# A graph network in one program: the fourth dense tile of a chunk is built in the attention stage instead of the message stage

## The reference

```python
h = relu(layernorm(x)); x = x + L0(h)   # messages: agg[src] += h[dst] * filter(edge) * cut
h = relu(layernorm(x)); x = x + L1(h)   # attention: softmax over the edges of each dst
h = relu(layernorm(x)); x = x + L2(h)   # graph convolution with degree norms
h = relu(layernorm(x)); x = x + L3(h)   # two weighted convolutions: out[dst] += ew * h[src]
```

## Time and profile before

| what | value |
|---|---|
| median of 3 runs | 5158.31 us (5143.35 to 5161.18) |
| the profiled execution | 5153.6 us, span 5151.8 us |
| mean granted TensorE clock | 0.901 of full |
| busy share of the span | PE 80%, PEld 68%, POOL 66%, DVE 59%, ACT 35% |
| message stage, about 130 to 1785 us | PE 1390.94, DVE 1155.84, ACT 965.19, POOL 1281.80 us busy; clock 0.94; DMA share 0.83 |
| attention stage, about 1985 to 3065 us | PE 893.86, DVE 819.86, ACT 419.71, POOL 774.95 us busy; clock 0.83; DMA share 0.23 |

### The profile page before, as it was taken

The page is one execution under the profiler, slowest core; times in us unless marked ns, Lnnn a source line. Parts: engine busy times, 40 slices in busy tenths (PEclk is TensorE's granted clock), DMA queues, the critical chain, the costliest instruction groups (busy, mean ns, idle before and its releaser), DMA issues.

```text
span 5151.8 us, 85066 instructions
## 1 busy us (share of the span) xinstructions
PE 4103.2 (80%) x25393; PEld 3526.8 (68%) x25393; DVE 3026.5 (59%) x10842; ACT 1786.2 (35%) x4226; POOL 3385.3 (66%) x3028
## 2 busy tenths in 40 slices
PE   2988888888888654888888885788876999869997
PEld 1665666556666454777777774666675999869996
DVE  3786666667667536777777764444444444434445
ACT  2665555555555433333333433222222000100001
POOL 0777777777777815777777735767644777457773
PEclk8999999999999876888888877999997999989998
DMA  6898888788888642222222212211115887567884
GB/s 202 210 208 182 183 187 178 177 185 186 182 185 187 129 109 65 56 55 55 54 55 55 54 29 66 53 49 50 49 31 206 287 294 281 179 229 281 291 294 155
DMA packets 516297, 768.12 MB, mean 149 GB/s; under 512 B 139247, under 2 KB 430680, under 8 KB 502520
## 3 DMA queue, kind: packets, MB, share of 16 engines
q0 software_dynamic: 189696, 201.26, 21.8%
q10 hardware_dynamic: 128128, 383.42, 20.3%
q1 hardware_dynamic: 198008, 177.89, 12.8%
HBM read 545.25 MB, written 217.03 MB: 148 GB/s over the span
## 4 chain that ended last, share of the span: by engine, by line
PE 40%; DMA 19%; issue 17%; DVE 12%; POOL 7%; DVEq 2%; SPq 1%; ACT 1%; POOLq 0%; ACTq 0%
DMA sums<-G,idx 18%; PE psCD L1330 8%; PE psF L1330 7%; POOL sums L741 7%; PE psCD L1249 5%; PE psCD L1303 3%; PE psA L1239 3%; PE psE L1303 3%; PE psCD L1315 3%; PE psF L1315 3%; DVE S L1881 2%; DVE G L1790 1%; PE psCD L1254 1%; DVEq L509 1%; DVE early L1870 1%
## 5 line engine op out<-in xcount | busy, mean ns | idle before, releaser
L716 POOL DMA_INDIRECT G<-table,idx x1352 | 1283.6, 949 | 778.6 <-issue 598.7
L741 POOL DMA_INDIRECT sums<-G,idx x832 | 1312.7, 1578 | 444.9 <-issue 203.6
L698 POOL DMA_INDIRECT G<-table,idx x832 | 785.8, 945 | 288.6 <-issue 252.0
L1187 PE MATMUL psB<-arena 128*128 128x300 f32 x1664 | 581.4, 482 | 251.8 <-ACT stage L909 213.3
L1187 PEld LDWEIGHTS psB<-arena 128*128 128x128 f32 x1664 | 317.4, 213 | 435.7 <-issue 304.1
L1330 PE MATMUL psCD<-arena,stage 128*128 128x192 f32 x2548 | 438.6, 330 | 0.0
L1330 PE MATMUL psF<-arena,stage 128*128 128x192 f32 x2548 | 431.3, 326 | 0.0
L828 ACT ACTIVATE arena<-psB,dinv 128x128 f32<-128x128 f32 x84 | 23.0, 378 | 1172.2 <-PE psB L1109 1160.5
L1330 PEld LDWEIGHTS psCD<-arena,stage 128*128 128x128 f32 x2548 | 419.6, 193 | 0.0
L1330 PEld LDWEIGHTS psF<-arena,stage 128*128 128x128 f32 x2548 | 411.8, 190 | 0.0
L909 ACT COPY stage<-psB 128x300 f32<-128x300 f32 x832 | 325.3, 426 | 239.4 <-PE psB L1187 233.2
(11 more groups left out here) (293 smaller groups left out, 8386.3 us busy)
## 6 DMA issues: line engine op xcount, KB each, us to landing
arena<-adjacency ACTq DMA_DIRECT2D x104, 2400.0 KB
adjacency<-stage ACTq DMA_DIRECT2D x416, 300.0 KB
acc<-in_src_row SPq DMA_DIRECT2D x104, 512.0 KB
arena<-in_dst_row SPq DMA_DIRECT2D x104, 512.0 KB
G<-table,idx POOLq DMA_INDIRECT x2184
sums<-G,idx POOLq DMA_INDIRECT x832
sums<-arena SPq DMA_DIRECT2D x4, 3300.0 KB, 25.5
table<-stage SPq DMA_DIRECT2D x28, 448.0 KB, 3.0
```

Of the source, the lines that this page charges most:

```text
L698: pool.indirect_dma_start(G[st.r][:, t * width:(t + 1) * width], None, tables[n], bass.IndirectOffsetOnAxis(ap=idx[st.r][:, t:t + 1], axis ...
L716: pool.indirect_dma_start(G[at.r][:, t * D:(t + 1) * D], None, tables[n], bass.IndirectOffsetOnAxis(ap=idx[at.r][:, t:t + 1], axis=0)).the ...
L741: pool.indirect_dma_start(sums_dram[t % SUMS], bass.IndirectOffsetOnAxis(ap=idx[st.r][:, t:t + 1], axis=0), G[st.r][:, t * TW:(t + 1) * TW ...
L1187: M.matmul(build_ps_1[q], lo, keys[:, q * HKEYS:(q + 1) * HKEYS], start=True, stop=True).then_inc(built["counted"], 1)
```

## The change

`AHEAD` becomes 3. In the message stage one `early_tile_hots`, two `early_half` products, two `early_half_kept` copies and one `early_tile_stored` per chunk go away, and `early_tile_stored(2)` takes the place of `early_tile_stored(3)` behind the first copy of the next turn. In the attention stage each turn gets one pair of one-hots, two half products, two copies and one store. The late tile uses buffers that are free in that stage: `lohots` and `keyhots` for the one-hots, `kept_2` in the arena, and one PSUM bank (`psB[:, 0:HKEYS]`) for both halves in turn, so the second product waits for the copy of the first. The numbers of tiles, bytes and sums over the whole program stay as they are.

```diff
-AHEAD = 4
+AHEAD = 3
...
+        kept_2 = [arena[:, behind + 5 * CHUNK + k * KEYS:behind + 5 * CHUNK + (k + 1) * KEYS] for k in range(RING)]
+        build_ps_2 = psB[:, 0:HKEYS]
...
+        def late_tile(c, j):
+            return CHUNKS * AHEAD + c * (DENSE - AHEAD) + j
...
             walk(act, general, l0["over"],
-                 [(low_sums_kept, 1), (early_tile_stored(3), 1), (filter_ssp, 0), (high_sums_kept, 1),
+                 [(low_sums_kept, 1), (early_tile_stored(2), 1), (filter_ssp, 0), (high_sums_kept, 1),
                   (early_half_kept(0, 0), 0), (early_half_kept(0, 1), 0), (keep_rows, 0), (early_tile_stored(0), 0),
-                  (early_half_kept(1, 0), 0), (early_half_kept(1, 1), 0), (early_half_kept(2, 0), 0), (early_half_kept(2, 1), 0), (early_tile_stored(1), 0),
-                  (early_half_kept(3, 0), 0), (early_half_kept(3, 1), 0), (early_tile_stored(2), 0)],
+                  (early_half_kept(1, 0), 0), (early_half_kept(1, 1), 0), (early_half_kept(2, 0), 0), (early_half_kept(2, 1), 0), (early_tile_stored(1), 0)],
...
             walk(act, general, l1["added"],
-                 [(diagonals, 0), (exps, 1), (onehot_turned, 0), (node_sums, 1)],
+                 [(diagonals, 0), (late_half_kept(0, 0), 1), (exps, 1), (onehot_turned, 0), (late_half_kept(0, 1), 1),
+                  (late_tile_stored(0), 1), (node_sums, 1)],
...
+            def late_half(j, q):
+                def stage_(st):
+                    b = late_tile(st.c, j)
+                    pe.wait_ge(built["hot"], b + 1)
+                    pe.wait_ge(built["kept"], 2 * b + q)
+                    M.matmul(build_ps_2, lohots[b % 2], keyhots[b % 2][:, q * HKEYS:(q + 1) * HKEYS],
+                             start=True, stop=True).then_inc(built["counted"], 1)
...
-                  (filter_two, 0), (early_half(2, 0), 0), (early_half(2, 1), 0), (early_half(3, 0), 0), (early_half(3, 1), 0)],
+                  (filter_two, 0), (early_half(2, 0), 0), (early_half(2, 1), 0)],
...
             walk(pe, general, l1["added"],
-                 [(per_edge, 1), (masked_scores, 0), (sums_turned, 2), (weighted_rows, 1)],
+                 [(per_edge, 1), (masked_scores, 0), (sums_turned, 2), (late_half(0, 1), 1), (weighted_rows, 1),
+                  (late_half(0, 0), 0)],
...
-                  (same_source, 0), (early_tile_hots(2), 0), (messages, 0), (early_tile_hots(3), 0)],
+                  (same_source, 0), (early_tile_hots(2), 0), (messages, 0)],
...
             walk(dve, general, l1["added"],
-                 [(new_maxima, 1), (window_onehot, 0), (exponents, 1), (weights, 1), (merge, 2), (largest, 0)],
+                 [(new_maxima, 1), (window_onehot, 0), (late_tile_hots(0), 0), (exponents, 1), 
+                  (weights, 1), (merge, 2), (largest, 0)],
```

More of the change, by code:

```diff
@@ L926, in early_tile_stored, with late_half_kept, late_tile_stored, stage_ @@
                 return stage_
+            def late_half_kept(j, q):
+                def stage_(st):
+                    b = late_tile(st.c, j)
+                    half_kept(b, q, kept_2, build_ps_2)
+                return stage_
+            def late_tile_stored(j):
+                def stage_(st):
+                    tile_stored(late_tile(st.c, j), st.c, AHEAD + j, kept_2)
+                return stage_
             def all_stored(tiles_built):
@@ L1004, in _ @@
             walk(act, general, l1["added"],
-                 [(diagonals, 0), (exps, 1), (onehot_turned, 0), (node_sums, 1)],
+                 [(diagonals, 0), (late_half_kept(0, 0), 1), (exps, 1), (onehot_turned, 0), (late_half_kept(0, 1), 1),
+                  (late_tile_stored(0), 1), (node_sums, 1)],
                  [], [diagonals, onehot_turned, exps, node_sums], 1)
+            with act.If(general > 0):
+                pass
+            with act.Else():
+                all_stored(CHUNKS * DENSE)
             def dense_kept(n):
@@ L1657, in early_tile_hots, with late_tile_hots, stage_ @@
                 return stage_
+            def late_tile_hots(j):
+                def stage_(st):
+                    b = late_tile(st.c, j)
+                    tile_hots(b, bass.ds(st.c * TILES + AHEAD + j, 1), (lohots[b % 2], keyhots[b % 2]))
+                return stage_
             dve.wait_ge(sums_clear, 16 * SUMS)
```

## The result

The changed kernel takes 5068.33 us (median of 4 runs, 5063.92 to 5071.42) beside 5153.64 us (5143.35 to 5161.18) for the kernel before: a ratio of 0.9835 [0.9814, 0.9856], some 85 us faster. Of these 22 us, 15 are the attention stage, which was forecast to lose them and did not move. In the message stage the sum came out, but not from the parts that it was added up from: the main item was priced too high by about as much as another, put at nothing, was worth.

The account below looks back on a forecast made before the run. The prediction took POOL's scatters and their landings to bound the message stage. It summed -83 us there and +15 us in the attention stage to -68 us, forecasting 5090 us, range 5025 to 5165.

Parts of the forecast that it names:

- the main item: Message stage: loads released 0.69 us sooner shorten the scatters' wait, 0.6 us per chunk.
- What bounds the kernel: Message stage: POOL's scatters and their landings set the pace, 16.1 us per chunk, 1.35 us above POOL's own.
- First item: Message stage: without the pair the loads issue 0.69 us sooner, saving 0.6 us per chunk, bounds nothing to 1.1.
- The products and copies lie beside the wait for the scatters and save nothing by themselves: Message stage: removing two products (1.25 us) and two copies (0.86 us) per chunk saves nothing by itself.
- Second item: Message stage: a scatter no longer lengthened by the pair beside it saves 0.1 us per chunk, bounds 0 and 0.22.
- Third item: Message stage: one store fewer ahead of the critical scatter saves 0.1 us per chunk, bounds 0 to 0.90.
- The sum: Message stage: the three savings make 0.8 us per chunk, 83 us over 104 chunks, bounds 0 and 141 us.
- The attention stage (+15 us): Attention stage: added late work takes the mean turn from 10.26 to 10.4 us, +15 us, bounds -6 and +46.
- Rival A: Attention stage: POOL loses each pair's whole 0.69 us, +43 us, taking back the message stage's gain; 5159 us, chance 0.14.
- B: Message stage nearly reaches POOL's own pace (-125 us) and the attention stage's clock stays up; 5027 us, chance 0.16.
- C: Message stage: loads ahead of the last scatter lengthen its landing; 5285 us, or 5203 with a third; chance 0.06.
- D: Message stage: the wait hangs on the loads whenever they come, so the shift changes nothing; 5163 us, chance 0.08.

Follow-up runs that it names:

- delay back: Changed kernel with one PSUM copy, about as long as the pair of one-hots, at the pair's old place in the message stage: 5065.11 us, ratio 0.9815.
- products back: Changed kernel with the fourth tile's two products and two copies back in the message stage, without its own pair or store: 5123.28 us, ratio 0.9946.
- pair back: Changed kernel with a fourth pair of one-hots back in the message stage, into a buffer that nobody reads: 5087.66 us, ratio 0.9860.
- loads sooner: Changed kernel with the duplicate sums ahead of the next window's one-hot in the message stage, releasing the loads earlier: 5107.38 us, ratio 0.9894.
- pair behind the weights: Changed kernel with the attention stage's late pair of one-hots behind the weights instead of behind the window's one-hot: 5067.24 us, ratio 0.9827.

## Why the prediction came out

**What bounds the kernel:** right. POOL's scatters and their landings set the message stage; their idle time fell and with it the whole time.

**First item, the loads released sooner (0.6 us): by itself worth nothing.** The loads did move, by 0.70 us in the turn (from 8.53 us behind ScalarE's release in the earlier trace rows to 7.83 us, the median after). But "delay back" undoes just that and costs nothing. The turn of the earlier trace rows that ran on pace with its loads 1.07 us ahead was read as showing what the loads do, but its last store was also far off, 3.15 us ahead of the scatter (issued at 1047.41). The place of the loads does go with the wait: in the five kernels with over 20 such chunks, those with loads just behind the last scatter and no late store wait 0.52 to 0.86 us, and in the changed kernel 75 of 80 chunks are no longer of that kind. What took them away was not the 0.69 us alone. A waiting turn can also keep them there: it lets ScalarE go by a landing, from which POOL's last scatter follows 8.27 us and the loads 8.53 us later. Which of the two comes first is not shown.

**"The products and copies lie beside the wait for the scatters and save nothing by themselves": this step failed.** Put back, they bring back 0.58 us per chunk, nearly all of the idle time. A way is seen in the trace: ScalarE, which makes the copies, also issues the stores, and a copy ahead of a store can delay it. Before, and with products back, a store leaves ScalarE within 1.5 us ahead of the chunk's last scatter in 51 and 50 of 80 chunks, in the changed kernel in 4. That scatter lands 8.12 and 8.29 us after its start in the chunks with such a store, and 7.38 and 7.14 us in those whose last store lies 1.5 to 2.5 us ahead; the mean is 7.83 before, 7.85 with products back and 6.35 after. The place of the store was not moved by itself, so its share is seen, not isolated. Even with a store further off, "products back" lands 0.8 us later than the changed kernel: there the loads are just behind the scatter. And of the four chunks with a late store in the changed kernel three have their loads 1.7 to 2.3 us behind the scatter and land after 3.3 to 3.8 us: a late store with no loads near it lengthens nothing there.

**Second item, the pair beside a scatter (0.1, bounds 0 and 0.22): mis-sized.** It is worth 0.21 to 0.22 us, the upper bound, by the mean scatter of "pair back". The other pairs did not move onto another scatter.

**Third item, the store (0.1, bounds 0 and 0.90): mis-sized, with no fixed price.** The rows that it was priced from leave out the store of 783.46, which is nearer to the scatter than the one named. Alone it costs 0.40 us, with the pair nothing more; "products back" is, but for the pair, as slow as the kernel before without any fourth store.

**The sum** of 0.8 us per chunk was 0.82, by luck: 0.6 for the loads came to nothing, and the products and copies, put at nothing, to 0.58.

**The attention stage (+15 us): wrong by 15 us.** TensorE's standing came out as worked out (1.71 us; 1.7 forecast), and VectorE's pair takes its 0.70 us (2399.61 to 2400.31). But the short turn shown is 9.53 us, not 10.1 (9.71 on the mean; 9.58 before). The one-hot starts 2.58 us after the reduce (2.77 in the earlier trace rows), the exponents come 0.48 us later behind it, not 0.70, and from them to the next reduce it is 5.11 us, not 5.37: only 0.03 us of the pair are left. And 34% of the turns are long, not 20%; before they were 40 of 103, 39%, where the prediction worked out 43%. POOL's pace with the pair, forecast at 10.2 us, is 10.14 us.

**Rival A** does not hold. POOL loses 23 ns per gather, 0.18 us per turn, not 0.69. The rule of the Trainium skill ("SBUF — State Buffer", section "SBUF: two separate sides"), a lock for a whole instruction, would make it 0.69. The direction agrees, since the pair lengthens scatters and gathers and the PSUM copy hardly does (1558 beside 1552 ns); that the pair runs in the mode which the rule names, and the whole length, are shown by no run. **B** reached too far: the message stage stopped at 15.29 us, and no clock rose. **C** and **D** fall with the time; C's direction is shown by "loads sooner". (The chances of the forecast and B add up to 0.72, not 0.71.)

## What to carry over

Work that lies beside a wait can still take part in it: here two products and two copies were worth 0.58 us per chunk, on an engine that also issues DMAs. Before such work is priced at nothing, look at what that engine's queue issues just ahead of the transfer everyone waits for. A turn that happens to run on pace shows that pace is possible, not which of its differences made it so. A delay of the same length with no other effect tells a moved release from what was removed with it, but a median after it does not say where single turns went: count them. Work can be free where it takes the place of waits, but the next portion need not be.

## What the runs showed of the hardware

A VectorE pair of 0.70 us costs POOL's indirect DMAs 0.22 us per pair in the scatters ("pair back") and 0.18 us per turn in the gathers, and 0.06 us at another place in the turn ("pair behind the weights", 951 beside 944 ns). A VectorE copy out of PSUM of 0.68 us costs the scatters 0.05 us per chunk (1558 beside 1552 ns).

A scatter's landing depends on what is in flight around it: on the mean the last one of a chunk takes 4.26 us with the loads issued 4.8 us ahead of it and 6.35 us in the changed kernel. With the loads 0 to 0.5 us behind it and no store in the 1.5 us ahead it takes 7.38 us in "products back" and 7.39 us before; with such a store as well 8.30 and 8.22 us.

Five versions of the attention stage with quite different work in it, from none of the late tile to all, and the kernel before keep one mean turn of 10.24 to 10.27 us, with shorter short turns mostly paid for by more long ones, in which the granted clock is at its lower level for a time.
